# Linear attention in a one-core decoder: four written-out batches with two sets of buffers in place of a loop over one set

## The reference

```python
qkv = jnp.einsum('btc,ec->bte', x, Wqkv) + bqkv
q, k, v = jnp.split(qkv, 3, axis=-1)
q = jax.nn.elu(q * scale) + 1.0          # heads of 8 columns
k = jax.nn.elu(k * scale) + 1.0
kv = k * v
k_cumsum = jnp.cumsum(k, axis=1)
kv_cumsum = jnp.cumsum(kv, axis=1)
denom = jnp.einsum('bthd,bthd->bth', q, k_cumsum)
denom = jnp.clip(denom, EPS, None)[..., None]      # EPS = 0.001
y = q * kv_cumsum / denom
return jnp.einsum('btc,ec->bte', y, Wproj) + bproj
# then x = _layernorm(x + result)
```

## Time and profile before

| | |
|---|---|
| median of 3 runs | 5208.85 us (5207.91 to 5213.28) |
| profiled execution, its own time | 5211.14 us |
| span of the profile | 5209.3 us |
| mean granted clock of TensorE | 0.881 of 2.4 GHz |
| busy in the span: PE, DVE, ACT, POOL | 4082.8, 3267.1, 2659.0, 1243.4 us |
| `finish` ahead: last store into `x_transposed` starts | 2793.49 us |
| linear attention, first product of the first batch to the last move to `outT` | 2797.11 to 2882.34 us |
| `finish` behind: first turning product | 2883.44 us |

### The profile page before, as it was taken

The page is one execution under the profiler, slowest core; times in us unless marked ns, Lnnn a source line. Parts: engine busy times, 40 slices in busy tenths (PEclk is TensorE's granted clock), DMA queues, the critical chain, the costliest instruction groups (busy, mean ns, idle before and its releaser), DMA issues. The chain is left out here.

```text
span 5209.3 us, 126790 instructions
## 1 busy us (share of the span) xinstructions
PE 4082.8 (78%) x45549; PEld 2393.4 (46%) x45678; DVE 3267.1 (63%) x5972; ACT 2659.0 (51%) x5482; POOL 1243.4 (24%) x2886
## 2 busy tenths in 40 slices
PE   2005767876669897696996588999999999999997
PEld 1003333432332222343442236777777777777775
DVE  7995444544437676434555426777777777777775
ACT  2035723544547676451221345666666666666664
POOL 0011200111101111110000144444444444444443
PEclk6557977987779899797997678999999999999998
DMA  2000020000000000002440001000000000000000
GB/s 56 0 0 1 2 73 18 1 1 1 4 30 1 1 2 1 11 1 77 139 138 28 5 1 50 6 10 24 6 27 6 6 28 6 10 24 6 28 6 11
DMA packets 60831, 110.20 MB, mean 21 GB/s; under 512 B 11399, under 2 KB 43251, under 8 KB 59164
## 3 DMA queue, kind: packets, MB, share of 16 engines
q1 hardware_dynamic: 59558, 101.70, 6.7%
q0 software_dynamic: 784, 1.80, 0.2%
HBM read 96.06 MB, written 1.74 MB: 19 GB/s over the span
## 5 line engine op out<-in xcount | busy, mean ns | idle before, releaser
L676 DVE TENSOR_REDUCE minus_max<-banks 128x1 f32<-128x512 f32 (+4 forms) x1152 | 606.3, 570 | 320.1 <-PE banks L571 313.8
L641 ACT ACTIVATE probs<-banks 128x512 f32<-128x512 f32 (+4 forms) x1152 | 581.1, 556 | 337.9 <-PE banks L609 335.4
L2862 POOL TENSOR_TENSOR loc_cos_part<-loc_cos_part,loc_sin_part 128x512 f32<-128x512 f32 x388 | 494.4, 1274 | 672.0 <-DVE loc_sin_part L3291 671.4
L2935 PE MATMUL banks<-loc_w_qkv,loc_shifted 128*128 128x256 f32 x1552 | 391.7, 396 | 15.3 <-DMA loc_adder_of<-loc_head_ones 14.8
L609 PE MATMUL banks<-q_stack,k_stack 64*128 64x512 bf16 (+3 forms) x1152 | 254.1, 381 | 98.5 <-DMA q_stack<-max_rows 70.8
L3324 DVE TENSOR_TENSOR loc_headsT<-banks,loc_sum_inv 128x512 f32<-128x512 f32 x192 | 132.7, 691 | 291.7 <-ACT loc_sum_inv L3196 291.7
L2935 PEld LDWEIGHTS banks<-loc_w_qkv,loc_shifted 128*128 128x128 f32 x1552 | 282.1, 192 | 55.2 <-DMA loc_w_qkv<-in_L_ffn_Wqkv_dram 15.2
L622 PE MATMUL banks<-probs,pair_rows 128*32 128x512 f32 (+3 forms) x2304 | 295.6, 589 | 0.0
L3316 DVE TENSOR_REDUCE loc_minus_max<-banks 128x4 f32<-128x384 f32 x386 | 197.1, 552 | 152.1 <-PE banks L3002 151.3
L700 POOL CAST max_parts<-minus_max 128x8 bf16<-128x8 f32 x192 | 36.3, 189 | 1042.2 <-DVE minus_max L676 1042.2
L1888 PE MATMUL banks<-identity,srt_b 128*128 128x128 f32 x64 | 11.2, 320 | 344.6 <-DVE srt_b L2168 344.6
(11 more groups left out here) (520 smaller groups left out, 9408.0 us busy)
## 6 DMA issues: line engine op xcount, KB each, us to landing
expert_share<-limited_rows SPq DMA_DIRECT2D x136, 256.0 KB, 3.9
expert_w<-in_L_ffn_pairs_dram SPq DMA_DIRECT2D x84, 192.0 KB, 2.3
loc_w_qkv<-in_L_ffn_Wqkv_dram SPq DMA_DIRECT2D x7, 1536.0 KB, 7.8
expert_share<-grouped_rows SPq DMA_DIRECT2D x32, 256.0 KB, 4.1
q_stack<-max_rows SPq DMA_DIRECT2D x384, 3.0 KB
loc_v_edge<-loc_v SPq DMA_DIRECT2D x192, 32.0 KB, 1.7
fixed_w<-in_L_ffn_experts_dram SPq DMA_DIRECT2D x8, 514.5 KB, 3.6
loc_pack<-in_L_ffn_pack_dram SPq DMA_DIRECT2D x6, 537.5 KB, 4.0
```

What stands on the lines that cost most here:

```text
L641: nc.scalar.activation(probs[(a % 2) * C + k][e][0:kn, q0:S], t_bank[e][0:kn, q0:S], ACT.Exp, scale=scale).then_inc(s["exp_done"], 1)
L676: nc.vector.tensor_reduce(minus_max[:, u, e, qs[0]:qs[0] + len(qs)], view, AX.X, ALU.max, negate=True).then_inc(s["max_done"], 1)
L2862: nc.gpsimd.tensor_tensor(cos_part[:, tiles, :], cos_part[:, tiles, :], sin_part[:, tiles, :], ALU.add).then_inc(s["summed"], 1)
L2935: ins = nc.tensor.matmul(g.bank[3 * j][:, (t % 2) * QK:(t % 2 + 1) * QK], xs[:, t * P:(t + 1) * P], w_qkv[:, ds(at, QK)], start=True, stop ...
```

## The change

The stage's functions are rewritten. There are two buffers of each kind (index `b % 2`), the loops are gone and the four batches are written out, and the order of each engine's queue is now given by small functions that are called in a chosen order. `numer` and `inverse` are buffers of their own. The products of q, k and v use banks 0 to 2 for even batches and 3 to 5 for odd ones; the denominator has bank 6 and the projection bank 7.

Work moves from DVE to ACT: the three steps `lin` (bias, and for q and k the scale) are ACTIVATE instructions, with the bias multiplied by the scale once at the start (`scaled_bias`), and the reciprocal is a logarithm and an exponential of its negative on ACT. The small block that set `ones` is gone; the memset is DVE's second instruction in the main block. The block has 19 named semaphores and `held` to clear, where it had 10 and `held`. Of the diff, with every function that sets the new order:

```diff
-        load(nc, g, [], ones=(ones[:, :],))
...
             def _(pe):
-                with pe.Fori(0, B) as b:
...
+                project_in(0)
+                project_in(1)
+                for b in range(B):
+                    denominator(b)
+                    if b + 2 < B:
+                        project_in(b + 2)
+                    if b:
+                        project_out(b - 1)
+                project_out(B - 1)
...
+                def linear(b):
+                    if b > 1:
+                        act.wait_ge(s["kv_done"], b - 1)
+                    for j in range(3):
+                        act.wait_ge(s["qkv_ready"], b * 3 + (j + 1))
+                        if j < 2:
+                            nc.scalar.activation(lin[b % 2][j][:, :], g.bank[(b % 2) * 3 + j][:, :], ACT.Identity,
+                                                 bias=scaled[:, j:j + 1], scale=columns[:, 4:5]).then_inc(s["lin_done"], 1)
...
+                def invert(b):
+                    act.wait_ge(s["above_done"], b + 1)
+                    nc.scalar.activation(above[b % 2][:, :], above[b % 2][:, :], ACT.Ln).then_inc(s["log_done"], 1)
+                    act.wait_ge(s["log_done"], b + 1)
+                    if b > 1:
+                        act.wait_ge(s["y_done"], b - 1)
+                    nc.scalar.activation(inverse[b % 2][:, :], above[b % 2][:, :], ACT.Exp,
+                                         scale=-1.0).then_inc(s["inverse_done"], 1)
...
+                linear(0)
+                linear(1)
+                exps(0)
+                for b in range(B):
+                    if b + 1 < B:
+                        exps(b + 1)
+                    if b + 2 < B:
+                        linear(b + 2)
+                    invert(b)
+                    if b:
+                        store(b - 1)
+                store(B - 1)
...
-                        if j < 2:
-                            nc.vector.tensor_scalar(lin[j][:, :], g.bank[j][:, :], columns[:, j:j + 1],
-                                                    columns[:, 4:5], ALU.add, ALU.mult).then_inc(s["lin_done"], 1)
...
+                def lower(b):
+                    dve.wait_ge(s["lin_done"], b * 3 + 2)
...
-                    step(nc.vector.tensor_scalar(above[:, :], g.bank[3][:, :], SMALL, None, ALU.max))
-                    step(nc.vector.reciprocal(above[:, :], above[:, :]))
-                    nc.vector.tensor_tensor(kv[:, :], feat[0][:, :], kv_sum[:, :], ALU.mult).then_inc(s["y_done"], 1)
...
+                lower(0)
+                for b in range(B):
+                    if b + 1 < B:
+                        lower(b + 1)
+                    sums(b)
+                    if b:
+                        result(b - 1)
+                    floor(b)
+                    numerator(b)
+                result(B - 1)
```

More of the change, by code:

```diff
@@ L1681, in linear_attention_3 @@
         outT = sbuf("outT", [P, T])
[L1682 to L1686, removed]
+        lin = [[sbuf(f"lin_{n}{u}", [P, S]) for n in "qkv"] for u in range(2)]
+        low = [[sbuf(f"low_{n}{u}", [P, S]) for n in "qk"] for u in range(2)]
+        feat = [[sbuf(f"feat_{n}{u}", [P, S]) for n in "qk"] for u in range(2)]
+        kv, k_sum, kv_sum, match, above, inverse, numer, y = (
+            [sbuf(f"{n}{u}", [P, S]) for u in range(2)]
+            for n in ("kv", "k_sum", "kv_sum", "match", "above", "inverse", "numer", "y"))
         ones = sbuf("ones", [P, S])
-        load(nc, g, [], ones=(ones[:, :],))
-        s = signals(nc, stack, "qkv_ready", "lin_done", "low_done", "exp_done", "chain", "match_done", "denom_ready",
-                    "y_done", "out_ready", "out_done")
+        scaled = sbuf("scaled_bias", [P, 2])
+        s = signals(nc, stack, "ones_done", "bias_done", "qkv_ready", "lin_done", "low_done", "exp_done", "feat_done",
+                    "kv_done", "k_sum_done", "match_done", "kv_sum_done", "denom_ready", "above_done", "log_done",
+                    "inverse_done", "numer_done", "y_done", "out_ready", "out_done")
         with nc.Block() as block:
@@ L1713, in _, with store @@
+                def store(b):
                     act.wait_ge(s["out_ready"], b + 1)
-                    nc.scalar.activation(outT[:, ds(b * S, S)], g.bank[4][:, :], ACT.Identity,
+                    nc.scalar.activation(outT[:, b * S:(b + 1) * S], g.bank[7][:, :], ACT.Identity,
                                          bias=columns[:, 3:4]).then_inc(s["out_done"], 1)
+                act.wait_ge(s["bias_done"], 1)
+                linear(0)
+                linear(1)
+                exps(0)
@@ L1717, in _ @@
+                for b in range(B):
[4 more added lines that the diff above has]
+                    invert(b)
+                    if b:
+                        store(b - 1)
+                store(B - 1)
             @block.vector
             def _(dve):
[L1719 to L1722, removed]
-                        if j < 2:
-                            nc.vector.tensor_scalar(lin[j][:, :], g.bank[j][:, :], columns[:, j:j + 1],
-                                                    columns[:, 4:5], ALU.add, ALU.mult).then_inc(s["lin_done"], 1)
[L1726 to L1729, removed]
-                    for j in range(2):
[L1731 to L1741, removed]
-                    dve.wait_ge(s["denom_ready"], b + 1)
-                    step(nc.vector.tensor_scalar(above[:, :], g.bank[3][:, :], SMALL, None, ALU.max))
-                    step(nc.vector.reciprocal(above[:, :], above[:, :]))
-                    nc.vector.tensor_tensor(kv[:, :], feat[0][:, :], kv_sum[:, :], ALU.mult).then_inc(s["y_done"], 1)
-                    dve.wait_ge(s["y_done"], b * 2 + 1)
-                    nc.vector.tensor_tensor(y[:, :], kv[:, :], above[:, :], ALU.mult).then_inc(s["y_done"], 1)
@@ new lines, in numerator, with floor @@
+                def numerator(b):
+                    u = b % 2
+                    dve.wait_ge(s["kv_sum_done"], b + 1)
+                    if b > 1:
+                        dve.wait_ge(s["y_done"], b - 1)
+                    nc.vector.tensor_tensor(numer[u][:, :], feat[u][0][:, :], kv_sum[u][:, :],
+                                            ALU.mult).then_inc(s["numer_done"], 1)
+                def floor(b):
+                    dve.wait_ge(s["denom_ready"], b + 1)
+                    if b > 1:
+                        dve.wait_ge(s["inverse_done"], b - 1)
+                    nc.vector.tensor_scalar(above[b % 2][:, :], g.bank[6][:, :], SMALL, None,
+                                            ALU.max).then_inc(s["above_done"], 1)
@@ new lines, in result @@
+                def result(b):
+                    dve.wait_ge(s["inverse_done"], b + 1)
+                    dve.wait_ge(s["numer_done"], b + 1)
+                    if b > 1:
+                        dve.wait_ge(s["out_ready"], b - 1)
+                    nc.vector.tensor_tensor(y[b % 2][:, :], numer[b % 2][:, :], inverse[b % 2][:, :],
+                                            ALU.mult).then_inc(s["y_done"], 1)
+                nc.vector.tensor_tensor(scaled[:, :], columns[:, 0:2], columns[:, 4:5].to_broadcast([P, 2]),
+                                        ALU.mult).then_inc(s["bias_done"], 1)
```

58 lines of the change are left out of this document (49 added, 9 removed).

## The result

| | before | after |
|---|---|---|
| median of the runs | 5209.8 us (5207.91 to 5213.28, 4 runs) | 5176.68 us (5174.01 to 5178.65, 4 runs) |
| profiled execution, its own time | 5211.14 us | 5174.01 us |
| last store of the `finish` ahead, end | 2794.09 | 2795.14 |
| lead: store's end to first product | 3.02 | 1.30 |
| body: first product to end of last move | 85.23 | 47.64 |

The median before holds one run more than the one that the forecast started from. "Body", "lead" and "tail" are used in this sense from here on. In the profiles the stage, lead and tail included, is 38.8 us shorter (89.35 less 50.53); the medians are 33.1 apart.

What follows compares the result with a forecast made beforehand. No engine is full; one single-file chain, about 21 us a batch, bounds the stage. Lead 1.43 + body 51.8 + tail 1.6 = 54.8 instead of 89.35 us, 34.5 less: 5208.85 - 34.5 = 5174.3 us, range 5166 to 5183.

Steps and rivals of the forecast that it cites:

- Lead: From the last store into `x_transposed` to the stage's first product: 1.43 us, without the block for `ones`, instead of 3.02.
- Tail: From the last move's end to the next `finish`: 1.6 us, between 1.1 and 2.1 for clearing 20 semaphores.
- Step 1: Body's start, six products in one run, four at half clock: `match` of batch 0 ends at 14.3 us.
- Step 2: From `match` of batch 0 to that of 1, and again from 1 to 2: 10.75 us each.
- Step 3: From `match` of batch 2 to that of batch 3, with no more products behind it: 7.0 us.
- Step 4: Body's end, from the last batch's denominator through inversion, `y` and projection to the last move: 9.0 us.
- of the rivals the first: PE's clock stays up: body 44.3 us, time 5166.8, with full clock from the first denominator on; chance 0.15.
- What lies beside: Work beside the body's path: three of four inversions hidden, only the last table load on it, DVE fullest (33 of 52 us).
- The costly switch: Rival: a switch of tables on ACT costs more than its row, 5.8 us more, 5180.1; chance 0.10.
- The single file: Rival: the stage's batches do not overlap, four of 22.1 us make 88, time 5211, no change; chance 0.02.
- Slower code behind the stage: Rival: later queues lie elsewhere in instruction memory; 0.24 us more a round in the last sublayer gives 5220; chance 0.02.
- my own sign of being wrong: Outside the stage: the forecast is wrong if other sublayers shift by more than a microsecond or two.

## Why the prediction was right, and where its steps were off

The forecast was 5174.3 us, the median came out at 5176.68, inside the range. The mechanism is the one forecast: the batches overlap, the chain from match to match runs through PE's products and ACT's move, and only the last table load is on it.

**Lead.** 1.43 reckoned, 1.30 measured. **Tail.** 1.6 reckoned, 1.59 measured; with the 14 semaphores of the reciprocal on ACT in the loop it was 1.27, with 11 it was 1.10. So a semaphore costs 0.05 to 0.06 in these three, and the 0.11 I had from the earlier trace rows was too much; the middle between my ends was right by luck.

**Step 1** (first match at 14.3) came at 12.3 and 12.7. The term that was mis-sized is the clock: I had four products at half step and the run had nearer to two (the rise at 3.0 and 3.8 us, a product taking 1.70 at half clock). **Step 2** (10.75 each) came as 10.2 and 9.7, and 10.4 and 10.3 in the second profile, by the same cause. **Step 3** (7.0) was 6.45, since the clock was still up for the denominator of batch 2 (1.12 us), and DVE never waited in it. **Step 4** (9.0) was 9.04. The sum was 51.8 and is 47.64 or 48.82, so of the rivals the first has its part: the clock was neither up throughout (43.25 when it nearly was) nor as low as before. The same walk with the clock rising sooner gave the bodies of the experiments ahead of their runs. Near ones: 70 for 70.43, 46.3 for 46.36, 42.7 for 43.25, 38.8 for 38.24, and the low ends of two ranges, 55 (to 57) for 54.84 and 44 (to 47.7) for 44.11. Farther ones: 79 to 80 for 77.77, 49.3 for 51.15, 42.4 for 40.25.

**What lies beside.** "Only the very last load is on the path" held to 0.01 us. "The first inverse comes only at 26.1, but DVE asks for it at 26.1 too" held in its order: the inverse came at 22.8 and DVE took it at 23.5, with no idle time in front of that `y`. DVE was not the fullest engine by itself, as I had said; ACT has 30.83 us to DVE's 29.82.

**The rivals.** The costly switch falls by two experiments. The single file exists only where it is made by hand, and its 70.43 is well under the 88 reckoned for it, because with two buffers PE makes the next products while DVE and ACT still work; I had put them back into the file. Slower code behind the stage is not seen: from the `finish` behind it to the last sublayer there pass 234.3 and 233.8 us, before 234.1 and 233.8. The rival was about the last sublayer, and there PE waits for its own issue as long as before; the line of the changed kernel, where L3125 is what was L3026:

```profile
PEld banks L3125 <- issue: 95.0, 161, 0.8
```

From the first turning product of `finish` to the end of the span there are 2325.9 and 2326.0 us in the two profiles of before and 2326.4 and 2325.9 in those of the change.

**What stays open.** The stage gained 38.8 and 37.6 us in the profiles, 3 to 4 more than my terms gave, but the medians only 33.1 and 34.7. My total was near the mark by luck in part: an error in the body (4 us too long) was met by one that I had no term for. The last store ahead of the stage ended at 2794.09 and 2794.17 in the two profiles of before, at 2795.14 and 2796.25 in those of the change, and between 2791.55 and 2803.10 in ten other kernels, in sublayers whose instructions were the same in all. Some microseconds come or go there from kernel to kernel, and my own sign of being wrong, other sublayers that shift by more than a microsecond or two, is met at its edge. For the profiled executions this closes the account. With the second profiles, 37.6 less the 2.1 by which the store ended later is 35.5, and the executions are 5211.28 - 5175.8 = 35.5 apart. With the first, 38.8 less 1.05 ahead and 0.6 behind is 37.2, and they are 5211.14 - 5174.01 = 37.1 apart; the other 4 us to the medians are that the change's profiled execution was the fastest of its four and that of before lay 1.3 above its median. Why the time ahead of the stage differs, whether by the place of the code in memory or by chance, was not tried.

## What to carry to other kernels

Where one chain of small steps runs over several engines, walk the queue of each engine forward with durations from the trace: with the clock as a profile had it, it told the bodies of nine variants, 38 to 78 us long, to within 2.2 us. The order of the queues was worth more here than the cost of any instruction, and the next gain was again an order (products ahead of the denominator). A table load mattered here only where the engine had no idle time to take it in (one of eight in this stage), and two functions that share a set should have that set preloaded, looking also at the sublayers behind.

## What was not expected of the hardware

The rise of TensorE's clock came 5.5 us behind the first of a run of products in the kernel before, and 3.0 and 3.8 us in two executions of the changed kernel, where the pause ahead of the run was 3.65 us in the first case and 1.93 in the others. The shorter pause is no full account of it. Of the ten profiles with a pause of 1.93, the changed kernel's two among them, seven have the rise at 2.9 to 3.0 us, one at 3.8, and two late: with the products ahead at 5.9, and in the kernel with the moves back on DVE 5.8 us behind the first product at 2799.30, as two stretches of it show:

```profile
2799.30:2805.00 5.70, 5.70 (x7) 2.49 (x8) 2.47 (x5) 0.00 (x0) 0.00 (x0) 0.50 0.00 0
2805.00:2806.00 1.00, 1.00 (x3) 0.38 (x2) 1.00 (x3) 0.09 (x1) 0.00 (x0) 0.93 0.00 0
```

The kernel before repeats its stage to 0.03 us and with it its clock, while the changed kernel does not. Nor does PE's queue of before fix it: with the reciprocal on ACT the rise came at 5.4, and with nothing added but the preload on ACT at 4.7, the pause being 3.65 in both. What else sets the moment was not found.

The preload of one table set shortened a sublayer that it does not stand in by 11 to 12.6 us, as 16 loads of 1.28 us there became needless. They had been 20.5 us of ACT, so somewhat over half of them lay on the path.
